# The gates' absolute value on ScalarE, a running sum that subtracts, and weight foldings behind the masks

## The reference

```
igate = concat(q, k, v) @ ig_kernel + ig_bias        # q from x, k = v = ctx
fgate = concat(q, k, v) @ fg_kernel + fg_bias
log_fg = log_sigmoid(fgate);  cums = cumsum(log_fg)
log_D[s, t] = cums[s] - cums[t] + igate[t]   (t <= s)
D = exp(log_D - max_t log_D);  C = (q k^T / sqrt(64)) * D
h = C / (max(|sum C|, exp(-max_log_D)) + 1e-6) @ v;  x = x + layernorm(h) * outnorm_weight   (before it, x is normalised)
n1 = layernorm(x); two attentions with 16 heads of 16 (wq, wk, wv, wo), mixed by a router's softmax
n2 = layernorm(x); router softmax, top 2 of 8 experts: gelu(n2 @ w1) @ w2, weighted sum
```

## Time and profile before

| | us |
|---|---|
| median of 3 runs | 1423.28 (1422.08 to 1424.86) |
| the profiled execution | 1428.74 |
| its span, first to last instruction | 1426.9 |
| TensorE's granted clock, mean over the span | 0.99 of full |
| TensorE busy | 1393.6 (98%) |
| VectorE / ScalarE / GpSimd busy | 1092.2 / 916.4 / 363.6 |

### The profile page before, as it was taken

How to read it: one execution, slowest core, us unless ns; L and a number is a source line. 1 busy time by engine, 2 the same in 40 slices (tenths; PEclk the granted TensorE clock), 3 DMA queues, 4 the chain that set the end, 5 groups by cost and what they waited for, 6 DMA issues and landing times.

```text
span 1426.9 us, 22218 instructions
## 1 busy us (share of the span) xinstructions
PE 1393.6 (98%) x7666; PEld 716.9 (50%) x7666; DVE 1092.2 (77%) x2299; ACT 916.4 (64%) x1706; POOL 363.6 (25%) x351
## 2 busy tenths in 40 slices
PE   8999899999999999999999999999999999999999
PEld 5643434455454654555445554455545454454456
DVE  5779977987789877987779877797769986786721
ACT  3266557766677666675677765876666766757752
POOL 6512342203313123132241133130331322330000
PEclk9999999999999999999999999999999999999999
DMA  4056037430854127441464308541084413561002
GB/s 116 17 70 95 2 45 107 71 62 16 104 76 76 45 38 112 75 75 31 51 101 69 64 31 101 79 75 46 24 102 70 78 56 45 73 77 46 17 1 89
DMA packets 92308, 90.15 MB, mean 63 GB/s; under 512 B 16483, under 2 KB 87267, under 8 KB 91295
## 3 DMA queue, kind: packets, MB, share of 16 engines
q1 hardware_dynamic: 92196, 88.73, 38.6%
HBM read 35.05 MB, written 4.25 MB: 28 GB/s over the span
## 4 chain that ended last, share of the span: by engine, by line
PE 69%; issue 8%; DVE 4%; DMA 3%; SPq 2%; POOL 1%; ACT 1%; DVEq 0%; POOLq 0%; ACTq 0%
PE psum L881 12%; PE psum L866 12%; PE psum L851 12%; PE psum L819 7%; PE psum L838 6%; PE psum L701 5%; PE psum L452 5%; PE psum L736 3%; DMA qst<-mrow 3%; PE psum L475 2%; SPq L1954 2%; PE psum L563 2%; DVE mx L1378 1%; PE psum L573 1%; DVE x L1293 1%
## 5 line engine op out<-in xcount | busy, mean ns | idle before, releaser
L1378 DVE TENSOR_REDUCE mx<-psum 128x1 f32<-128x512 f32 x1024 | 645.5, 681 | 134.2 <-PE psum L851 133.5
L1677 ACT ACTIVATE prob<-psum 128x512 f32<-128x512 f32 x1024 | 568.2, 600 | 270.8 <-PE psum L881 159.4
L866 PE MATMUL psum<-qst,kst 98*128 98x512 bf16 x1024 | 355.9, 383 | 10.5 <-DMA qst<-mrow 8.7
L851 PE MATMUL psum<-kst,qst 96*128 96x512 bf16 x1024 | 318.8, 381 | 2.9 <-DVE resid L1252 1.3
L881 PE MATMUL psum<-prob,vst 128*17 128x512 f32 x2048 | 248.1, 601 | 2.7 <-ACT prob L1677 2.3
L866 PEld LDWEIGHTS psum<-qst,kst 98*128 98x128 bf16 x1024 | 96.9, 99 | 220.8 <-issue 126.9
L851 PEld LDWEIGHTS psum<-kst,qst 96*128 96x128 bf16 x1024 | 99.0, 98 | 121.2 <-issue 17.9
L881 PEld LDWEIGHTS psum<-prob,vst 128*17 128x17 f32 x2048 | 46.7, 97 | 136.3 <-issue 106.8
L838 PE MATMUL psum<-w,cxT 128*128 128x256 f32 x448 | 105.4, 381 | 0.0
L819 PE MATMUL psum<-n2T,x 128*128 128x512 f32 x224 | 103.0, 592 | 0.0
L1828 POOL CAST parts<-resid 128x512 bf16<-128x512 f32 x64 | 41.0, 640 | 239.9 <-DVE resid L1252 239.9
(11 more groups left out here) (244 smaller groups left out, 1761.5 us busy)
## 6 DMA issues: line engine op xcount, KB each, us to landing
kst<-parts SPq DMA_DIRECT2D x186, 128.0 KB, 4.7
qst<-parts SPq DMA_DIRECT2D x186, 128.0 KB, 5.9
cmat<-G_dram SPq DMA_DIRECT2D x7, 1024.0 KB, 4.6
x<-in_L_ffn_fw SPq DMA_DIRECT2D x14, 512.0 KB, 3.7
w<-in_L_ffn_fw SPq DMA_DIRECT2D x14, 512.0 KB, 4.2
xbuf<-in_x SPq DMA_DIRECT2D x8, 512.0 KB, 5.1
kin<-in_ctx SPq DMA_DIRECT2D x8, 512.0 KB, 4.5
out<-acc SPq DMA_DIRECT2D x7, 512.0 KB, 9.0
```

The costliest lines, as they stand in the source:

```text
L851: e.matmul(psum[:, u.bank, :], qst[0:KROWS, h, t * P:(t + 1) * P], kst[0:KROWS, h, :], start=True, stop=True).then_inc(u.full, 1)
L866: e.matmul(psum[:, u.bank, :], kst[0:KROWS + 2, h, g * P:(g + 1) * P], qst[0:KROWS + 2, h, :], start=True, stop=True).then_inc(u.full, 1)
L1378: e.tensor_reduce(mx[:, qq * QUAD + j, t:t + 1], psum[:, u.bank, :], AX, ALU.max).then_inc(u.free, 1)
L1677: e.activation(prob[:, g % 2, j, :], psum[:, u.bank, :], ACT.Exp).then_inc(u.free, 1)
```

## The change

- ScalarE's first gate instruction becomes Abs of the forget gates (tile ga), Exp takes scale -1, and Ln stays. The copy of the input gates now writes partitions 0 to 3 directly and stands behind Ln; it waits for gn, since the bank is read there too.
- VectorE makes gn = min(f + bias, 0) from PSUM, and the running sum adds gn and subtracts Ln's result in one scan. L982 and L986 are gone. g waits for the bank's release by the input gates' copy.
- The gate row's DMA, its semaphore and SP's piece gi are gone.
- wk's folding uses tensor_copy and stands behind the masks with the five small preparations; wq's is on ScalarE (fold_q), behind the last mask's exponents of batch 0.
- keep_clock(20) behind the gates' matmuls becomes keep_clock(14).
- load_x(1) waits for batch 0's statistics.
- All three plans are replaced, with CARRY, MADE, COPY and SENT.

More of the change, by code:

```diff
@@ L159, in build @@
         cmat = sb("cmat", [P, NH, S])
-        gi, gf, ga, lf = (cmat[0:NH, r, :] for r in range(4))
-        gi_made = cmat[GI:GI + NH, 0, :]
+        gi, gn, ga, gf = (cmat[0:NH, r, :] for r in range(4))
         AW = NH * (DH + 1)
@@ L315, in build @@
             POOL_C={},
[L316 to L317 removed]
+            POOL_S=slots(0, "s3:0 s4:7 s5:9 s6:11 s7"),
+            SP_A=slots(-7, "ctx:21 x:5 G:51 s0:25 s1:16 s2:0 s3"),
             SP_C={},
[L319 to L321 removed]
+            SP_S=slots(4, "s3:2 s4:11 s5:20 s6:11 s7"),
@@ L322, in build @@
+            AHEAD="4241400202000122302024032004101310111130302022221000000200120000"
+                  "2011124000000000201222040002020230030100021111110010401001000000")
         MIDDLE = dict(
[L323 to L327, removed]
@@ L347, in build @@
[L347 to L350, removed]
+            PE_A=slots(3, "kT0:2 kT1:5 qT0:0 qT1 gates:2 gsum:17 cols:14 cd0:2 cd1:6 st0:0 st1:0 st2:2 num0 num1:8 "
+                       "num2:0 num3:22 n1T0:2 n1T1 p0:4 p1:2 p2:7 p3 pv0:23 pv1:0 logits"),
+            PE_C=slots(2, "cxT00:5 cxT01:6 cxT10:0 cxT11 wo0:0 wo1:4 wo2:3 wo3:23 mean:0 n2T0:3 n2T1:3 logits:9 "
+                       "hid00:0 hid01 hid02 hid03 eo00:6 eo01:0 eo02:2 eo03:5 hid10:0 hid11 hid12:0 hid13:2 eo10:6 "
+                       "eo11:2 eo12:7 eo13"),
@@ new lines, in build @@
+            PE_S=slots(4, "p4 p5:17 p6 p7:12 v0 v1"),
+            DVE_A=slots(2, "bn0 bn1:0 bn2:0 bn3 var:2 qn0:0 qn1 qn2:0 qn3:5 gn:2 F g:4 G M:9 cols:0 gend:10 dec:5 "
[3 rows of a table added]
+            DVE_C=slots(14, "wo0:0 wo1:4 wo2:2 wo3:2 bn0:2 bn1:3 bn2:0 bn3:4 var:3 n20:0 n21:0 n22:2 n23:11 mean:5 "
+                        "logits:2 topk:8 acc00:6 acc01:0 acc02 acc03:10 acc10:4 acc11:3 acc12:7 acc13"),
+            DVE_S=slots(6, "s4:0 s5:16 s6 s7"),
+            ACT_A=slots(4, "kT0:2 kT1:4 qT0:0 qT1 gpart:2 grow1 fa:0 grow0:17 mask00:0 mask01:0 mask02:0 mask03:2 "
+                        "mask10:0 mask11:2 mask12:0 mask13:0 mask20:3 mask21:0 mask22:0 mask23 mask30:0 mask31:2 "
+                        "mask32 mask33:0 decexp:22 sq0:0 sq1:22 n1T0 n1T1:0 p0:5 p1:2 p2:6 p3:2 pv0:23 pv1:0 logits"),
@@ new lines, in build @@
+            ACT_C=slots(2, "cxT00:5 cxT01:6 cxT10:0 cxT11:31 n2T0:3 n2T1:4 logits:8 hid00:0 hid01:2 hid02:0 hid03:14 "
+                        "hid10 hid11:0 hid12:0 hid13"),
+            ACT_S=slots(5, "p4:0 p5:16 p6 p7:13 v0 v1"),
+            POOL_A=slots(3, "pw:29 vcopy:3 mask0 mask1:10 mask2:6 mask3:0 vw:17 hw:14 hs:19 hn:8 x2:3 r1:3 r5 s0:10 "
+                         "s1:0 s2:0 s3"),
+            POOL_C=slots(23, "acc0:7 r1"),
+            POOL_S=slots(11, "s4:0 s5:16 s6:13 s7"),
+            SP_A=slots(0, "ctx:0 x:21 G:56 s0:14 s1:6 s2:26 s3"),
@@ L351, in build @@
+            SP_C=slots(51, "w10:0 w20:17 w11:6 w21:35 out"),
+            SP_S=slots(13, "s4:8 s5:12 s6:17 s7"),
+            AHEAD="4112100010223023103300300001010202401022011100011010000100424411"
+                  "1001010021421300110204131022113111000112011021010112010011000000")
         LAST = dict(
             PE_A={},
-            PE_C=slots(5, "cxT00:3 cxT01:2 cxT10 cxT11:2 wo0 wo1 wo2:3 wo3:22 mean:7 n2T0:0 n2T1:3 logits:9 hid00 "
-                       "hid01:0 hid02:0 hid03 eo00:8 eo01 eo02:6 eo03:2 hid10:51 hid11:2 hid12:0 hid13:0 eo10:2 "
+            PE_C=slots(7, "cxT00:3 cxT01:3 cxT10 cxT11:0 wo0:5 wo1:3 wo2:4 wo3:6 mean:15 n2T0:0 n2T1:4 logits:10 hid00 "
+                       "hid01:0 hid02 hid03:3 eo00:2 eo01 eo02:7 eo03:2 hid10:51 hid11:2 hid12:0 hid13:0 eo10:2 "
```

80 lines of the change are left out of this document (31 added, 49 removed), and 14 rows, old and new, of tables (DVE_A, va).

## The result

The changed kernel takes 1431.6 us (median of 6 runs, 1429.9 to 1434.8) against 1423.9 for the kernel before in the same comparison (6 runs, 1422.1 to 1426.2). The ratio is 1.0057, with a 95% interval of 1.0043 to 1.0070. I had forecast 1419.9, with 1425.5 as the upper end.

The account below looks back on a forecast made before the run. TensorE is busy 98% of the span, so the gain was priced in batch 0's gates chain: 0.89 + 0.71 + 1.07 + 1.03 = 3.70; 1423.3 - 3.7 + 0.3 = 1419.9 us, range 1415.5 to 1425.5.

Parts of the forecast that it names:

- Steps 1, 2 and 4: Batch 0's gates: Abs on ScalarE saves 0.89 us, dropping L986 0.71, no POOL contention on VectorE 1.03.
- Step 3: Batch 0's gates: ScalarE writes the input gates' row in place, so the wait for its DMA goes, 1.07 us less.
- the first rival: Prologue: TensorE's clock holds during the spreads of G, some 2.8 us earlier, giving 1417.1; chance 0.27.
- I cost this at 0: Middle periods: VectorE's 0.67 us less per batch changes no PE wait; priced at 0, with -6 as a bound.
- Net 0.3: First period: four more ctx transposes ahead of batch 0's first projection cost 0.44 to 0.55 us, 0.1 to 0.2 returned.
- one rival: No gain: Abs needs its own table, or replanned first period and ending give 3 us back, 1422 to 1424; chance 0.13.
- The second rival: POOL's make_x3 ahead of the next batch's splits stretches VectorE's n1q; at 1 us per period 1426.9; chance 0.15.
- The right side, slower: Whole kernel slower by over 0.2%: most of the second rival and some of the plan's risk; chance 0.14.
- The foldings: Prologue: wk's folding on POOL behind the masks (0.66 us each) and fold_q on ScalarE (1.6 to 2.8) are hidden.

Follow-up runs that it names:

- c1: The kernel before, unchanged, run again for a second profile; 1423.9 us.
- a1: The changed code under all three plans and the constants of the kernel before; 1438.9 us, ratio 1.011 to the kernel before.
- d1: b3 with five rows of the first plan (PE_S, DVE_S, ACT_S, POOL_S, SP_S) as in the kernel before; 1437.3 us, ratio 1.01.
- d3: b2 with the foldings of the kernel before, so that the gates' chain alone is changed; 1423.0 us, ratio 1.0003.
- b2: Changed code with the input gates' copy ahead of Exp for batches 1 to 7, under the plans and constants of before; 1422.9 us, ratio 0.9995.
- b1: The kernel before with only the input gates' copy moved behind Ln for batches 1 to 7; 1450.4 us, ratio 1.0179.
- b3: The changed kernel, new plans kept, with the input gates' copy ahead of Exp for batches 1 to 7; 1431.0 us, ratio 1.0048.
- a2: The code of the kernel before under the three new plans and constants; 1432.8 us, ratio 1.0078.
- c3: b2 with the new first plan alone; middle plan, last plan and constants as before; 1430.8 us, ratio 1.0061.
- c2: b3 with VectorE's running sum, g and running maximum of batch 1 spread over later slots of the first plan; 1431.2 us, ratio 1.0073.

## Why the prediction was wrong, step by step

**The steps of the gates.** Steps 1, 2 and 4 came out in the profile as worked out: 0.89 and 0.71 gone, and g, the scan and M back at 0.68, 1.21, 0.68. b4, with the foldings alone moved, has the same three durations. The Trainium skill's rule on who interferes with whom (SBUF — State Buffer) agrees with c1 again: the same three instructions take 0.95, 1.55 and 0.92 there while POOL folds.

**Step 3's size.** 1.07 us was the wait in one execution; c1 shows 0.1. Against c1, M's end moves from 23.8 to 21.4, so by 2.4 and not by 3.5, and the first scores by 2.2. The same execution gave the first rival its 2.8 us: the clock did hold in the changed kernel's profile, but it held in c1 as well, and it fell with the new chain in a1, d1 and d3. I had noted that the profiled execution was 5.5 above the median and still took differences from it, because "the chain's instructions repeat to a few ns where nothing disturbs them". Instructions do; a DMA's landing and the clock do not, and two of my items hung on those.

**Step 3's other end: a term at nothing that is not nothing.** I moved the gate row's copy behind Ln, priced the copy and its reader, and never asked what the copy releases. The text says of the middle periods: "ScalarE's count is the same, so are its table loads. No PE wait hangs on either", "I cost this at 0". The first half is right. The second was read from a kernel in which the bank was free after 1.9 us. In its place: the bank is held for 4.4 us (6.9 in a1) in batch 1, and the wait recurs in the middle periods. This is worth 16 us with the old plans (a1 less b2) and 27 in the kernel before (b1). Under the plans of the change it is worth 0.6, not told from nothing (the changed kernel less b3), so it is not where the changed kernel's own 8 us went.

**The plans: the failed step.** The sum has the new plans at "Net 0.3", and one rival, with a chance of 0.13, has "the replanned first period and ending" at up to 3 us. They cost 8 us on the mended code (b3 less b2) and 10 on the code of before (a2), nearly all in the first plan (c3). What I did price there, kT1's four transposes ahead of the first projection, is in the timeline at about its price: the eight take 1.06 at 53.79. The loss stands later, between the first scores and context 0, in a stretch that I did not walk through: the send of the maxima comes 2.7 later, TensorE stands still for 3.8 us more, and its clock falls behind the longest wait, which adds most of another 2.6. Which entry of the plan makes the send late stays open.

**How these add up.** Under the old plans: 1423 for before, 0 for the mended change (b2), +16 for the held bank, 1438.9 (a1). The new plans take 7.3 of that back, as their waits for the copy are short (1.0 us in five middle periods against 8.5), and leave 1431.6. Taken the other way round: 1423, 0 for the mended change, +8 for the new plans (b3), 0.6 for the copy's late place. The middle period is 167.10 in both kernels, as the sum had it; that it stays so only under the new middle plan did not show in it.

**The second rival**, POOL's make_x3 in front of the splits, has no part in it: no wait for n1q stands among those of PE, and the middle periods kept their length. The stretching that it feared is there, though: the n1q normalisations (L1129, 32 of them) take 0.40 to 1.92 us, median 0.48, where they took 0.40 to 0.41 before (L1133). The right side, slower, had 0.14, most of it for this rival. The "some of the plan's risk" in it was the true reason, held to be at most 3 us.

**The foldings** were hidden, as worked out: wk takes 2.30 for four (0.57 each, I took 0.66), fold_q 2.36 for four, POOL then idles 2.56 before the gain, ScalarE 5.30. Rows of the changed kernel, against the earlier trace rows:

```profile
29.80 2.30 POOL L1864 COPY wk<-x 128x256 f32<-128x256 f32 x4
36.19 1.18 POOL L1806 TENSOR_TENSOR kin<-qbuf,onw 128x512 f32<-128x512 f32 x1 [2.56 <-DVE nrm L1186]
...
28.48 2.36 ACT L1589 ACTIVATE wq<-acc 128x256 f32<-128x256 f32 x4
36.13 0.63 ACT L1535 ACTIVATE kT<-qbuf 128x512 f32<-128x512 f32 x1 [5.30 <-DVE qbuf L1085]
```

## What to carry to other kernels

For each instruction that is moved later, write down what it releases, not only what it computes: the last reader of a PSUM bank that TensorE takes in fixed turn sets when TensorE may go on, and a 0.68 us copy cost 16 to 27 us here under the plans of before. A plan of slots is fitted to one set of releases: judge code and plan apart, by running each with the other's partner, before blaming either. Here the crossed runs were needed to see that the held bank, though real, is not what slows the changed kernel. And where a gain hangs on a DMA's landing or on the clock, take a second profile of the kernel before: a single one put 1.0 us too much into this sum and all of its 2.8 us into a rival.

## What the runs showed of the hardware that I had not expected

- The clock's fall in the prologue is not in every execution of the same code: 0.50 between 28 and 32 us in the first profile, 1.00 in c1.
- A long wait of TensorE can cost twice. Behind waits of 4.07 us (a1, b1), 3.23 (b3) and 1.95 (the changed kernel) the clock fell to the 1.2 GHz level for some us, and TensorE was busy for 2.6 to 3.6 us more up to context 0 than in b2 or c1. Behind 2.64 (c2) and 1.01 (b2) it stayed at 1.00, so the length of that one wait does not decide it.
- One small DMA (the moved gate row) was issued at 17.57 in one execution of the kernel before and at 17.06 in the other, and its reader started at 21.29 and at 20.31: 1 us, 0.51 of it in the issue and the rest in the way.
- Four permuted copies of 256 elements take POOL 0.57 each as tensor copies, where the multiplying form took 1.05 to 1.16 each; the same on ScalarE takes 0.59.
- Abs on ScalarE needs no table load beside Exp. The Trainium skill (ScalarE: Activation LUTs, "Table sets") says that abs is in every set, and the trace agrees: Exp starts at 14.69, 0.03 behind Abs.
- Every version with the foldings moved took 2.1 to 2.3 us outside the span in each of its runs, every version without 1.7 to 1.9. b2 and d3 differ in nothing else (2.1 to 2.2 against 1.7 to 1.8), so moving the foldings adds 0.4 to 0.5 us there. Whether fold_q or wk's tensor copies do it is not told apart.
